# Four heads to a key transpose, read out by ScalarE's scale and bias, and a gate-up product that stays in PSUM

## The chip, the core and the metric

The kernel runs on one core of a Trainium2 chip. The metric is the device time of one execution, in microseconds (us).

## What is computed

A block of 16 batches of 256 tokens of width 256, in fp32:

```
x = x + attention(layernorm(x), keys and values from fside; ctx gives 256 more keys and values)   # 16 heads of 16
x = x + sum over 8 experts e of cw[e] * (silu(h @ w_gate[e]) * (h @ w_up[e])) @ w_down[e]          # h = layernorm(x)
```

Every expert is applied to every token (hidden width 1024); cw is a product of two softmaxes over the experts, normalised. So the expert part is by far the largest: for each group of two batches (512 tokens), 8 experts times 8 blocks of 128 hidden units.

## The kernel before

**Precision.** Most matmul operands are split into a high and a low fp32r part, and a product takes three passes (high by high, high by low, low by high). The high part is a ScalarE copy, the low part a subtraction on VectorE (DVE) or GpSimd (POOL).

**Steps and turns.** The program is one unrolled list of turns of 32 steps. In turn b the engines do the attention of batch b, prepare batch b+1, close batch b-1, and, from step 19 of turn 2 on, one expert block f in each step. There are 512 such blocks. Every engine walks the same steps in order and waits on semaphores; nothing is reordered at run time.

**One step on TensorE (PE)**, in this order: gate(f+1), six matmuls into `ps_g` (L660, shown as ps_s); up(f+1), six into `ps_u` (L660, ps_t); down(f), six into `ps_o` (L694); every fourth step the attention-times-value matmuls (L735, L737); one "misc" item by the table ITEMS; the scores of item i+8 for their maximum (L753), the transposed scores (L763).

**One step on ScalarE (ACT):** tanh of the gate into the SBUF tile `hf` (L777); one or two weight halves (L789); `h_hi`, a copy of `hf` (L782); parts of the values' split; the read-out of the misc item; the exponential `Pt` (L916). **On DVE:** (tanh+1)*gate into `hf` (L937); times up, into `hf` (L944); statistics; `h_lo` = `hf` - `h_hi` (L949); the router's small operations; in even steps `Pt_lo`, the low part of the exponentials (L1077; POOL has the others, L1237); the misc item; the negated row maximum `negmax` (L1141), which frees the one score bank. **On POOL:** low weight halves (L1172), `kstack`'s low parts, the sum over experts.

**The locks that matter here.** tanh(f+1) waits for h_lo(f), which is the last reader of `hf`. up(f+1) waits for the product (L944) of f, the last reader of `ps_u`. down(f) waits for h_lo(f). All misc items share one PSUM bank, `ps_m`, so each waits until the one before has been read out.

**Keys.** The split keys lie in `kstack` as four slots of 16 columns per head: high, low, a slot that is 1.0 in three columns, high again. A misc item "kT" transposes two heads (128 columns) for each of four key tiles into `ps_m` (L597), and one ScalarE copy of 128x512 brings it to `KTs` (L888). The ones meet three rows of `QTs` that carry the query's maximum. Eight kT items per batch stand in steps 19, 20, 25, 27, 28 of the turn before and 0, 1, 4 of the batch's own. A "qq" item does the same for the queries and ends in four ScalarE copies, two of 3x256 (L899) and two of 64x256 (L904).

Of the kernel before, what the change touches and what calls it, by code (L numbers as in the profile page):

```python
# [29 lines left out]
P = 128  # L30
# [6 lines left out]
def bass_xattn_moe_ffn_kernel(nc, x, ctx1, ctx2, Wq, bq, Wk, bk, Wv, bv, Wp, bp, w_router, w_gating,  # L37
# [52 lines left out]
    with ExitStack() as ctx:  # L90
# [130 lines left out]
        qT_ps = Count("qT_ps", 8); qT_done = Count("qT_done", 16)  # L221
        kT_ps = Count("kT_ps", 8); kT_done = Count("kT_done", 8)
        v_1 = Count("v_1", 4); v_r = Count("v_r", 4); v_2 = Count("v_2", 4); v_3 = Count("v_3", 4)
# [22 lines left out]
        class Turn:  # L246


            def __init__(self, b):
                self.b = b  # L250
                self.closed = (b - CLOSED) // GB if b >= CLOSED and (b - CLOSED) % GB == 0 else None
                self.qs_at, self.ks_at, self.ms_at = (10, 8, 5) if b == -1 else (18, 12, 13)

# [21 lines left out]
        def turns(body):  # L275

            for b in range(-2, LAST + 1):
                body(Turn(b))

        ITEMS = [(0, "kT", 5, 0), (1, "kT", 6, 0), (2, "qq", 1, 0), (3, "cT", 0, 1), (4, "kT", 7, 0), (5, "aT", 0, -1),  # L280
# [4 lines left out]

        FIRST_AT = {"cT": (1,), "xT": (2,), "kv": (4, 6), "q": (9,)}

        def q_ahead(k, d):

            return (k + 2) % PAIRS, d + (k + 2) // PAIRS  # L290

        def released(b, name, k, d):

            turn = Turn(b)
            if name == "y":
# [5 lines left out]
            count, nth = {"kT": (kT_done, k + 1), "kv": (kv_done, k + 1), "xT": (xT_l, 1), "cT": (cT_l, 1), "aT": (aT_l, 1),  # L301
                          "x2T": (x2T_l, 1), "q": (q_done, 1), "o": (x1_done, 1), "lg": (ldif_done, 1),
                          "cwT": (cwT_done, 1)}[name]
            return [(count.sem, (b + d) * count.per + nth)] if turn.has(d) else []
# [119 lines left out]
        def _(eng):  # L424
# [22 lines left out]
            def body(turn):  # L447
                for step in range(STEPS):
# [20 lines left out]
                    if step == 24 and turn.has(-1):  # L469
                        turn.wait(eng, cwT_done, -1, 1)  # L470
                        eng.dma_start(d_cw[:, bass.ds((turn.b - 1) * N, N)], cwT[:]).then_inc(cw_out.sem, 16)
# [67 lines left out]
        def _(pe):  # L539
# [21 lines left out]
            def stack_block(stack, t, pair):  # L561
                return stack[:, t * H + 2 * pair:t * H + 2 * pair + 2].rearrange("p h s d -> p (h s d)")

            def do_misc(turn, name, k, d, one, freed):
                ps = bank(one)
# [23 lines left out]
                elif name == "kT":  # L589
# [9 lines left out]
                    mm.then_inc(kT_ps.sem, 1)  # L599
                elif name == "qq":  # L600
                    if turn.has(d):
# [106 lines left out]
            def body(turn):  # L708
                for step in range(STEPS):
# [36 lines left out]
                    if turn.has(d):  # L746
                        h, qt = i // QT, i % QT
                        if i % 4 == 0:
                            turn.wait(pe, kT_done, d, h // 2 + 1)
                            turn.wait(pe, qT_done, d, 2 * (h // 2) + 2)  # L750
# [20 lines left out]
        def _(act):  # L771

            def tanh_of(f):

                act.wait_ge(g_ps, f + 1)
                wait_for(act, hl_done, f)
                act.activation(hf[:], ps_g[:], ACT.Tanh, scale=0.5).then_inc(tanh_done, 1)  # L777

            def high_of(f):

                act.wait_ge(hf_done, f + 1)
                act.activation(h_hi[f % FC][:], hf[:], ACT.Copy).then_inc(hh_done, 1)  # L782

# [16 lines left out]
            def before_ffn():  # L800
# [11 lines left out]
                           ACT.Copy).then_inc(const_ready, 1)  # L812

            def split_high(n):

                hi, raw = parts[n]
                act.wait_ge(w_in[n], 32 if n == 4 else 16)
                act.activation(hi, raw, ACT.Copy).then_inc(w_high, 1)

            def body(turn):  # L820
                for step in range(STEPS):
                    f = turn.f(step)
# [17 lines left out]
                    if step == turn.ks_at and turn.has(1):  # L840
                        turn.wait(act, kv_done, 1, QT)
                        turn.wait(act, kT_ps, 0, PAIRS)
                        act.activation(slots(kstack, 0, 0, 4, 3), heads_twice(KF), ACT.Copy).then_inc(ks_h.sem, 1)
                    if step == turn.ms_at and turn.has(1):
                        turn.wait(act, c2_in, 1, 16)
                        turn.wait(act, kT_ps, 0, PAIRS)
                        act.activation(slots(kstack, QT, 0, 4, 3), heads_twice(VF[:, QT:KC, :]),
                                       ACT.Copy).then_inc(ms_h.sem, 1)

# [35 lines left out]
                    if name == "kT":  # L885
                        turn.wait(act, kT_ps, d, k + 1)
                        turn.wait(act, t_ps, d - 1, 4 * k + 4)
                        act.activation(KTs[:, k, :], ps[:], ACT.Copy).then_inc(kT_done.sem, 1)  # L888
                    if name == "qq":
# [32 lines left out]
        def _(dve):  # L922
# [103 lines left out]
            def body(turn):  # L1026
                for step in range(STEPS):
# [6 lines left out]
                    for n in LOW_AT.get((turn.b, step), ()):  # L1034
                        split_low(n)
                    if turn.b == -1 and step == 8:
                        dve.wait_ge(b_in[0], 16)
# [32 lines left out]
                    if f is not None and f % EXPERT == EXPERT - 1:  # L1070
                        weigh_output(f, 1)
                    router_weights(turn, step)
                    d, i = item_at(step, -1)
                    if turn.has(d) and by_dve(i):
                        turn.wait(dve, exp_done, d, i + 1)
                        slot = i % RING
                        dve.tensor_tensor(Pt_lo[slot][:], Pt[slot][:], Pt[slot][:].bitcast(BF16)[:, 1::2],  # L1077
                                          ALU.subtract).then_inc(lo_dve.sem, 1)
                    name, k, d, one, _ = misc(turn, step)
# [57 lines left out]
                    if turn.has(d):  # L1137
                        turn.wait(dve, s_ps, d, i + 1)
                        if i % 4 == 0:
                            turn.wait(dve, mq_l, d, i // 4 - 1)  # L1140
                        dve.tensor_reduce(negmax[:, (i // 4) % 2, i % 4:i % 4 + 1], score_bank((turn.b + d) * STEPS + i)[:], AX.X, ALU.max,  # L1141
                                          negate=True).then_inc(max_done.sem, 1)

            turns(body)


        @block.gpsimd
        def _(pool):
# [46 lines left out]
            def body(turn):  # L1195
                for step in range(STEPS):
# [55 lines left out]
                    if step == turn.ks_at and turn.has(1):  # L1252
                        turn.wait(pool, ks_h, 1, 1)
                        pool.tensor_tensor(slots(kstack, 0, 1, 2, 1)[:, :, 0, :], heads(KF),
                                           slots(kstack, 0, 0, 1, 1)[:, :, 0, :].bitcast(F32),
                                           ALU.subtract).then_inc(ks_l.sem, 1)
                    if step == turn.ms_at and turn.has(1):
                        turn.wait(pool, ms_h, 1, 1)
                        pool.tensor_tensor(slots(kstack, QT, 1, 2, 1)[:, :, 0, :], heads(VF[:, QT:KC, :]),
                                           slots(kstack, QT, 0, 1, 1)[:, :, 0, :].bitcast(F32),  # L1260
                                           ALU.subtract).then_inc(ms_l.sem, 1)
                    f = turn.f(step)
# [36 lines left out]
```

## Time and profile before

| | |
|---|---|
| median of 3 runs | 2788.32 us (2787.05 to 2789.99) |
| the profiled execution | 2787.18 us, of it the span 2785.0 us |
| PE busy | 2719.2 us, 98% of the span |
| DVE / POOL / ACT busy | 2198.7 / 1807.1 / 1695.8 us (79 / 65 / 61%) |
| chain that ended last | PE 87%, DVE 6%, issue 3%, ACT 3% |

The profile covers one execution. A matmul's end is modelled, so records of consecutive matmuls overlap (0.39 us long, 0.23 us apart); what they cost is read from start to start. Times within the trace count from the start of the span.

### The profile page before, as it was taken

How to read it: one execution, taken by the hardware profiler on the slowest of the kernel's cores; microseconds unless marked ns; L12 is line 12 of the kernel's file. 1: busy time of each engine (PE TensorE's matmuls, PEld its weight loads, DVE VectorE, ACT ScalarE, POOL GpSimd, SP SyncE). 2: the span in 40 equal slices, each digit the busy share in tenths (PEclk: the TensorE clock that was granted, in tenths of full speed). 3: DMA queues.
4: the chain of work that ended last, by engine and by line, in shares of the span. 5: the costliest groups of instructions: out<-in, count | busy, mean ns of one | idle time of the engine just before them, and what ended most of it. 6: DMA issues, size and time to landing. Idle time of an engine off the chain costs nothing.

```text
span 2785.0 us, 47540 instructions
## 1 busy us (share of the span) xinstructions
PE 2719.2 (98%) x16416; PEld 2224.1 (80%) x16416; DVE 2198.7 (79%) x3254; ACT 1695.8 (61%) x3241; POOL 1807.1 (65%) x1886
## 2 busy tenths in 40 slices
PE   7789999999999999999999999999999999999998
PEld 5578878888888888878788787887878888888887
DVE  7977788878888788787787888878888878766665
ACT  7866566665666666566666666656666666644443
POOL 6766666666666667666676666766666666654554
PEclk8999999999999999999999999999999999999999
DMA  2113233332333323333232322323323233333332
GB/s 69 39 57 99 80 92 96 91 103 79 96 92 95 99 81 91 95 95 99 79 93 88 103 89 86 99 82 109 95 73 100 76 103 92 95 106 114 106 104 82
DMA packets 251275, 252.27 MB, mean 91 GB/s; under 512 B 15904, under 2 KB 242848, under 8 KB 251040
## 3 DMA queue, kind: packets, MB, share of 16 engines
q1 hardware_dynamic: 251040, 249.25, 29.9%
q8 instruction: 134, 2.20, 0.3%
q14 instruction: 101, 0.83, 0.1%
HBM read 240.66 MB, written 8.52 MB: 89 GB/s over the span
## 4 chain that ended last, share of the span: by engine, by line
PE 87%; DVE 6%; issue 3%; ACT 3%; POOL 1%; DMA 0%; POOLq 0%; ACTq 0%; DVEq 0%
PE ps_s L660 23%; PE ps_t L660 23%; PE ps_o L694 23%; PE ps_s L753 4%; PE ps_t L763 3%; PE ps_m L549 3%; PE ps_a L735 2%; PE ps_a L737 2%; DVE negmax L1141 1%; DVE h_lo L949 1%; DVE Pt_lo L1077 1%; PE ps_m L597 1%; PE ps_m L557 1%; DVE hf L944 1%; ACT h_hi L782 1%
## 5 line engine op out<-in xcount | busy, mean ns | idle before, releaser
L949 DVE TENSOR_TENSOR h_lo<-hf,h_hi 128x512 fp32r<-128x512 f32 x512 | 514.6, 1005 | 230.8 <-ACT h_hi L782 220.5
L782 ACT ACTIVATE h_hi<-hf 128x512 fp32r<-128x512 f32 x512 | 323.9, 633 | 522.0 <-DVE hf L944 522.0
L937 DVE SCALAR_TENSOR_TENSOR hf<-hf,ps_s 128x512 f32<-128x512 f32 x512 | 349.5, 683 | 268.5 <-ACT hf L777 265.4
L777 ACT ACTIVATE hf<-ps_s 128x512 f32<-128x512 f32 x512 | 306.0, 598 | 306.2 <-PE ps_s L660 200.9
L1172 POOL TENSOR_TENSOR wg_lo<-stage_w,wg_hi 128x512 fp32r<-128x512 f32 x256 | 338.8, 1323 | 223.2 <-ACT wg_hi L789 223.0
L1237 POOL TENSOR_TENSOR Pt_lo<-Pt 128x512 f16<-128x512 f32 x256 | 312.4, 1220 | 152.8 <-ACT Pt L916 152.5
L694 PE MATMUL ps_o<-h_hi,wd_hi 128*128 128x512 f32 x1024 | 399.9, 391 | 0.9 <-DVE h_lo L949 0.9
L694 PE MATMUL ps_o<-h_lo,wd_hi 128*128 128x512 f32 x1024 | 399.9, 391 | 0.0
L694 PE MATMUL ps_o<-h_hi,wd_lo 128*128 128x512 f32 x1024 | 398.6, 389 | 0.0
L1172 POOL TENSOR_TENSOR wd_lo<-stage_w,wd_hi 128x512 fp32r<-128x512 f32 x256 | 332.3, 1298 | 82.2 <-ACT wd_hi L789 82.0
L944 DVE TENSOR_TENSOR hf<-hf,ps_t 128x512 f32<-128x512 f32 x512 | 351.8, 687 | 35.5 <-PE ps_t L660 0.8
L916 ACT ACTIVATE Pt<-ps_t 128x512 f32<-128x512 f32 x512 | 304.2, 595 | 121.2 <-PE ps_t L763 117.2
L1172 POOL TENSOR_TENSOR wu_lo<-stage_w,wu_hi 128x512 fp32r<-128x512 f32 x256 | 366.6, 1432 | 0.0
L1141 DVE TENSOR_REDUCE negmax<-ps_s 128x1 f32<-128x512 f32 x512 | 346.2, 678 | 3.6 <-PE ps_s L753 3.5
L660 PE MATMUL ps_s<-xh,wg_hi 128*128 128x512 f32 x1024 | 323.6, 397 | 3.2 <-issue 3.2
L660 PE MATMUL ps_s<-xl,wg_hi 128*128 128x512 f32 x1024 | 319.4, 393 | 0.0
L660 PE MATMUL ps_s<-xh,wg_lo 128*128 128x512 f32 x1024 | 318.3, 392 | 0.0
L660 PE MATMUL ps_t<-xh,wu_hi 128*128 128x512 f32 x1024 | 318.0, 391 | 0.0
L660 PE MATMUL ps_t<-xh,wu_lo 128*128 128x512 f32 x1024 | 316.8, 391 | 0.0
L660 PE MATMUL ps_t<-xl,wu_hi 128*128 128x512 f32 x1024 | 315.2, 389 | 0.0
L1077 DVE TENSOR_TENSOR Pt_lo<-Pt 128x512 f16<-128x512 f32 x256 | 290.1, 1133 | 5.6 <-ACT Pt L916 5.5
L753 PE MATMUL ps_s<-KTs,QTs 128*128 128x512 f32 x512 | 235.4, 460 | 28.0 <-DVE negmax L1141 25.0
(190 smaller groups left out, 5117.6 us busy)
## 6 DMA issues: line engine op xcount, KB each, us to landing
stage_w<-in_L_ffn_w_gate_dram SPq DMA_DIRECT2D x256, 256.0 KB, 2.8
stage_w<-in_L_ffn_w_up_dram SPq DMA_DIRECT2D x256, 256.0 KB, 3.0
stage_w<-in_L_ffn_w_down_dram SPq DMA_DIRECT2D x256, 256.0 KB, 2.7
cwb<-d_cw SPq DMA_DIRECT2D x64, 256.0 KB, 3.8
X<-in_x_dram SPq DMA_DIRECT2D x32, 256.0 KB, 3.6
C<-in_fside_BxSxS_dram SPq DMA_DIRECT2D x16, 256.0 KB, 3.0
KVM<-in_ctx_dram SPq DMA_DIRECT2D x16, 256.0 KB, 2.7
d_x<-X SPq DMA_DIRECT2D x16, 256.0 KB, 2.4
```

The lines of the kernel that those rows point to most:

```text
L660: mm = pe.matmul(ps[:], wt[:, c, q * P:(q + 1) * P], tok[:, c].rearrange("p k n -> p (k n)"), start=(n == 0), stop=(n == 3 * DC - 1))
L694: mm = pe.matmul(ps_o[:, c, :], wt[:, q, c * P:(c + 1) * P], hid[:], start=(at == 0 and n == 0), stop=(at == EXPERT - 1 and n == 2))
L753: pe.matmul(score_bank(j)[:], QTs[:, h // 2 % QRING, h % 2, qt * P:(qt + 1) * P], KTs[:, h // 2, :], start=True, stop=True).then_inc(s_ps. ...
L777: act.activation(hf[:], ps_g[:], ACT.Tanh, scale=0.5).then_inc(tanh_done, 1)
L782: act.activation(h_hi[f % FC][:], hf[:], ACT.Copy).then_inc(hh_done, 1)
L937: dve.scalar_tensor_tensor(out=hf[:], in0=hf[:], scalar=1.0, in1=ps_g[:], op0=ALU.add, op1=ALU.mult).then_inc(gate_done, 1)
L944: dve.tensor_tensor(hf[:], hf[:], ps_u[:], ALU.mult).then_inc(hf_done, 1)
L949: dve.tensor_tensor(h_lo[f % FC][:], hf[:], h_hi[f % FC][:].bitcast(F32), ALU.subtract).then_inc(hl_done, 1)
L1077: dve.tensor_tensor(Pt_lo[slot][:], Pt[slot][:], Pt[slot][:].bitcast(BF16)[:, 1::2], ALU.subtract).then_inc(lo_dve.sem, 1)
L1141: dve.tensor_reduce(negmax[:, (i // 4) % 2, i % 4:i % 4 + 1], score_bank((turn.b + d) * STEPS + i)[:], AX.X, ALU.max, negate=True).then_in ...
L1172: pool.tensor_tensor(lo[:], raw_weights(n), hi[:].bitcast(F32), ALU.subtract).then_inc(wl_done, 1)
L1237: pool.tensor_tensor(Pt_lo[slot][:], Pt[slot][:], Pt[slot][:].bitcast(BF16)[:, 1::2], ALU.subtract).then_inc(lo_pool.sem, 1)
```

## The change

1. **A key transpose of four heads ("kQ"), for batches 3 to 15.** `kstack` holds only high and low (32 columns per head, the view `qkeys`), so 128 columns are four heads. The item fills `ps_m` with four heads; the slots doubled and the ones set are made while reading out. `keys_out` writes one pair of heads with four ScalarE instructions of 32x512: for each head a Copy of its 32 rows, and an Identity of the same 32 rows with `scale=high_rows` and `bias=max_rows` (one value for each partition, from SBUF), which gives ones and high. A second call in the next step (`keys_next`) writes the other pair. kQ stands in steps 12, 19, 27 of the turn before and 0 of its own. Batches 0 to 2 keep kT.
2. **The copies into the stack:** one half instead of two (L843, L847), in steps 10 and 11 instead of 12 and 13. Items o, kv, kv, xT move to steps 7, 8, 9, 11; y's second and cwT trade places (23, 24); the store of cwT moves to step 25.
3. **The product stays in PSUM:** L944 writes `ps_u` in place; h_hi and h_lo read it there. tanh(f+1) waits only for the product of f; up(f+1) waits for h_lo(f).
4. **DVE's order:** the router's operations and `Pt_lo` come last in the step, after `negmax`.

```diff
-        ITEMS = [... (8, "o", 0, -1), (9, "kv", 0, 1), (10, "qq", 3, 0), (11, "kv", 1, 1), (13, "xT", 0, 1),
+        ITEMS = [... (7, "o", 0, -1), (8, "kv", 0, 1), (9, "kv", 1, 1), (10, "qq", 3, 0), (11, "xT", 0, 1),
...
+                 (0, "kQ", 3, 0), (12, "kQ", 0, 1), (19, "kQ", 1, 1), (27, "kQ", 2, 1)]
...
+                elif name == "kQ":
+                    for t in range(KC):
+                        mm = pe.transpose(ps[:, t * P:(t + 1) * P].bitcast(F32R), quad_block(t, k), ident_r[:])
+                    mm.then_inc(kT_ps.sem, 2)
...
             def up(f):
-                wait_for(pe, hf_done, f)
+                wait_for(pe, hl_done, f)
...
             def tanh_of(f):
-                wait_for(act, hl_done, f)
+                wait_for(act, hf_done, f)
...
             def high_of(f):
-                act.activation(h_hi[f % FC][:], hf[:], ACT.Copy).then_inc(hh_done, 1)
+                wait_for(act, d_ps, DC * (f - 1))
+                act.activation(h_hi[f % FC][:], ps_u[:], ACT.Copy).then_inc(hh_done, 1)
...
+            def keys_out(turn, ps, pair, d):
+                turn.wait(act, t_ps, d - 1, 4 * pair + 4)
+                act.wait_ge(rows_ready, 2)
+                for h in range(2):
+                    src, dst = 2 * HD * (pair % 2 * 2 + h), HS * h
+                    act.activation(KTs[dst:dst + 2 * HD, pair, :], ps[src:src + 2 * HD, :], ACT.Copy).then_inc(kT_done, 1)
+                    dst = dst + 2 * HD
+                    act.activation(KTs[dst:dst + 2 * HD, pair, :], ps[src:src + 2 * HD, :], ACT.Identity,
+                                   bias=max_rows[src:src + 2 * HD, :], scale=high_rows[src:src + 2 * HD, :]).then_inc(kT_done, 1)
...
             def hidden_of(f):
-                dve.tensor_tensor(hf[:], hf[:], ps_u[:], ALU.mult).then_inc(hf_done, 1)
+                dve.tensor_tensor(ps_u[:], hf[:], ps_u[:], ALU.mult).then_inc(hf_done, 1)
...
             def low_of(f):
-                dve.tensor_tensor(h_lo[f % FC][:], hf[:], h_hi[f % FC][:].bitcast(F32), ALU.subtract).then_inc(hl_done, 1)
+                dve.tensor_tensor(h_lo[f % FC][:], ps_u[:], h_hi[f % FC][:].bitcast(F32), ALU.subtract).then_inc(hl_done, 1)
```

## Rows read from the trace of the kernel before

**Rows 1.** The page's first part: busy us (share) x instructions, by engine.
```profile
PE 2719.2 (98%) x16416; PEld 2224.1 (80%) x16416; DVE 2198.7 (79%) x3254; ACT 1695.8 (61%) x3241; POOL 1807.1 (65%) x1886
```
**Rows 2.** The waits of PE, 350 to 2350 us: us in total, times, longest.
```profile
PE ps_s L753 <- DVE negmax L1141: 16.3, 12, 1.6
```
**Rows 3.** The chain in time, steps 27 to 30 of turn 8: start, us, what.
```profile
1236.38 0.30 PE ps_m L597 x4
...
1237.20 1.40 PE ps_s L660 x6
...
1242.16 1.40 PE ps_s L660 x6
...
1246.76 1.40 PE ps_s L660 x6
...
1252.51 0.23 PE ps_s L660
```
**Rows 4.** ScalarE's timeline, turn 8, steps 19, 26 to 29: start, us, instruction.
```profile
1192.16 0.59 ACT L777 ACTIVATE hf<-ps_s 128x512 f32<-128x512 f32 x1
...
1231.75 0.78 ACT L899 ACTIVATE QTs<-ps_m 3x256 fp32r<-3x256 f32 x2 [0.68 <-PE ps_m L612]
1232.55 0.78 ACT L904 ACTIVATE QTs<-ps_m 64x256 fp32r<-64x256 f32 x2
1233.36 0.60 ACT L916 ACTIVATE Pt<-ps_t 128x512 f32<-128x512 f32 x1
1233.85 0.59 ACT L777 ACTIVATE hf<-ps_s 128x512 f32<-128x512 f32 x1
...
1235.92 0.63 ACT L782 ACTIVATE h_hi<-hf 128x512 fp32r<-128x512 f32 x1 [0.96 <-DVE hf L944]
1236.71 0.60 ACT L888 ACTIVATE KTs<-ps_m 128x512 fp32r<-128x512 f32 x1 [0.16 <-PE ps_m L597]
...
1238.64 0.60 ACT L777 ACTIVATE hf<-ps_s 128x512 f32<-128x512 f32 x1 [0.80 <-PE ps_s L660]
...
1243.60 0.60 ACT L777 ACTIVATE hf<-ps_s 128x512 f32<-128x512 f32 x1 [0.80 <-PE ps_s L660]
```
**Rows 5.** PE's timeline, turn 8: starts of gate in steps 19, 29, of up in 30.
```profile
1189.04 0.63 PE L660 MATMUL ps_s<-xh,wg_hi 128*128 128x512 f32 x2
...
1242.00 0.63 PE L660 MATMUL ps_s<-xh,wg_hi 128*128 128x512 f32 x2
...
1247.99 0.62 PE L660 MATMUL ps_t<-xh,wu_hi 128*128 128x512 f32 x2
```
**Rows 6.** DVE's timeline, step 29 of turn 8: h_lo.
```profile
1246.43 0.69 DVE L949 TENSOR_TENSOR h_lo<-hf,h_hi 128x512 fp32r<-128x512 f32 x1 [0.70 <-ACT h_hi L782]
```
**Rows 7.** DVE and PE in step 21 of turn 8, around the wait of Rows 2.
```profile
1202.83 1.53 DVE L1077 TENSOR_TENSOR Pt_lo<-Pt 128x512 f16<-128x512 f32 x1
1204.28 0.68 DVE L1141 TENSOR_REDUCE negmax<-ps_s 128x1 f32<-128x512 f32 x1
...
1205.01 0.50 PE L753 MATMUL ps_s<-KTs,QTs 128*128 128x512 f32 x1 [1.14 <-DVE negmax L1141]
```
**Rows 8.** Groups by line, whole span: busy us, mean ns of one | idle before.
```profile
L949 DVE TENSOR_TENSOR h_lo<-hf,h_hi 128x512 fp32r<-128x512 f32 x512 | 514.6, 1005 | 230.8 <-ACT h_hi L782 220.5
...
L866 ACT ACTIVATE lexp<-ldif 128x16 f32<-128x16 f32 x32 | 4.8, 198 | 0.0
```
**Rows 9.** DVE and PE near the end, steps without attention: h_lo, next up.
```profile
2704.61 1.47 DVE L949 TENSOR_TENSOR h_lo<-hf,h_hi 128x512 fp32r<-128x512 f32 x1 [0.70 <-ACT h_hi L782]
...
2705.67 0.62 PE L660 MATMUL ps_t<-xh,wu_hi 128*128 128x512 f32 x2
```
**Rows 10.** POOL's timeline, step 10 of turn 7: the sum over experts.
```profile
1145.06 3.45 POOL L1191 TENSOR_TENSOR acc<-acc,wout 128x512 f32<-128x512 f32 x2
```
**Rows 11.** SP's queue in turn 8, steps 24 and 25: the store of cwT, the first load back.
```profile
1217.02 0.30 SPq L471 DMA_DIRECT2D d_cw<-cwT  x1
...
1222.82 0.41 SPq L520 DMA_DIRECT2D cwb<-d_cw  x1
```

More of the change, by code:

```diff
@@ L57, in bass_xattn_moe_ffn_kernel @@
     DVE_LOW = (1, 3, 5, 7)
+    QUADS = PAIRS // 2
+    FIRST_QUAD = 3
     SCALE = float(HD) ** -0.5
@@ L290, in q_ahead, with by_quad, keys_done @@
             return (k + 2) % PAIRS, d + (k + 2) // PAIRS
+        def by_quad(b):
+            return b >= FIRST_QUAD
+        def keys_done(b, pairs):
+            late = max(b - FIRST_QUAD, 0)
+            return (b - late) * PAIRS + late * 2 * QT * PAIRS + pairs * (2 * QT if by_quad(b) else 1)
         def released(b, name, k, d):
             turn = Turn(b)
+            if name in ("kT", "kQ"):
+                if not turn.has(d) or by_quad(b + d) != (name == "kQ"):
+                    return []
+                return [(kT_done, keys_done(b + d, 2 * k + 2 if name == "kQ" else k + 1))]
             if name == "y":
@@ L468, in body @@
                         eng.dma_start(x1_v[:, bass.ds((turn.b - 1) * QT, QT), :], X1[:]).then_inc(x1_out.sem, 16)
-                    if step == 24 and turn.has(-1):
+                    if step == 25 and turn.has(-1):
                         turn.wait(eng, cwT_done, -1, 1)
@@ L842, in body @@
                         turn.wait(act, kT_ps, 0, PAIRS)
-                        act.activation(slots(kstack, 0, 0, 4, 3), heads_twice(KF), ACT.Copy).then_inc(ks_h.sem, 1)
+                        if by_quad(turn.b + 1):
+                            act.activation(qkeys[:, 0:QT * H, 1, :], heads(KF), ACT.Copy).then_inc(ks_h.sem, 1)
+                        else:
+                            act.activation(slots(kstack, 0, 0, 4, 3), heads_twice(KF), ACT.Copy).then_inc(ks_h.sem, 1)
                     if step == turn.ms_at and turn.has(1):
@@ L846, in body @@
                         turn.wait(act, kT_ps, 0, PAIRS)
-                        act.activation(slots(kstack, QT, 0, 4, 3), heads_twice(VF[:, QT:KC, :]),
-                                       ACT.Copy).then_inc(ms_h.sem, 1)
+                        if by_quad(turn.b + 1):
+                            act.activation(qkeys[:, QT * H:KC * H, 1, :], heads(VF[:, QT:KC, :]),
+                                           ACT.Copy).then_inc(ms_h.sem, 1)
+                        else:
+                            act.activation(slots(kstack, QT, 0, 4, 3), heads_twice(VF[:, QT:KC, :]),
+                                           ACT.Copy).then_inc(ms_h.sem, 1)
                     for o, at, d in v_at(turn):
@@ L887, in body @@
                         turn.wait(act, t_ps, d - 1, 4 * k + 4)
-                        act.activation(KTs[:, k, :], ps[:], ACT.Copy).then_inc(kT_done.sem, 1)
+                        act.activation(KTs[:, k, :], ps[:], ACT.Copy).then_inc(kT_done, 1)
+                    if name == "kQ":
+                        turn.wait(act, kT_ps, d, 2 * k + 2)
+                        keys_out(turn, ps, 2 * k, d)
+                    if keys_next:
+                        keys_out(turn, bank(keys_next[3]), 2 * keys_next[1] + 1, keys_next[2])
+                    keys_next = items[turn.b, step] if name == "kQ" else None
                     if name == "qq":
@@ L1035, in body @@
                         split_low(n)
+                    if turn.b == 0 and step == 0:
+                        in_head = ident[:].rearrange("p (a r) -> p a r", r=2 * HD)
+                        dve.tensor_reduce(high_rows[:], in_head[:, :, HD:2 * HD], AX.XY, ALU.add).then_inc(rows_ready, 1)
+                        dve.tensor_reduce(max_rows[:], in_head[:, :, 0:3], AX.XY, ALU.add).then_inc(rows_ready, 1)
                     if turn.b == -1 and step == 8:
@@ L1071, in body @@
                         weigh_output(f, 1)
[L1072 to L1078, printed above, removed]
                     name, k, d, one, _ = misc(turn, step)
@@ L1142, in body @@
                                           negate=True).then_inc(max_done.sem, 1)
+                    router_weights(turn, step)
+                    d, i = item_at(step, -1)
+                    if turn.has(d) and by_dve(i):
+                        turn.wait(dve, exp_done, d, i + 1)
+                        slot = i % RING
+                        dve.tensor_tensor(Pt_lo[slot][:], Pt[slot][:], Pt[slot][:].bitcast(BF16)[:, 1::2],
+                                          ALU.subtract).then_inc(lo_dve.sem, 1)
             turns(body)
```

30 lines of the change are left out of this document (20 added, 10 removed), and 6 rows, old and new, of the table ITEMS.

## The prediction

> **What bounds the kernel now.** First the page's busy times: PE is busy for 98% of the span, no other engine for more than 79% [rows 1]. Then PE's waits between 350 and 2350 us: there is one kind, the score matmul waiting for `negmax`, twelve times, once per turn in step 21 [rows 2]. So in steady state PE runs back to back but for one hole per turn, and the time is the sum of what PE streams. The chain gives that from start to start: a step without a misc item lasts 4.60 us (1242.16 to 1246.76), one with a kT item 4.96 (1237.20 to 1242.16), one with a qq item and the value matmuls 5.75 (1246.76 to 1252.51) [rows 3]. Last, ScalarE's and DVE's timelines, for the loop that feeds PE: gate, tanh, two DVE products, h_hi, h_lo. A faster step is worth something only while this loop keeps up.
>
> **What it saves.** (a) A kT item costs 4.96 - 4.60 = 0.36 us of PE's time: 0.30 of it are the four transposes, the rest the exposed load behind them [rows 3]. Thirteen batches have four items fewer each: 52 x 0.36 = 18.7 us, all of it on the path. (b) The hole in step 21: DVE spends 1.53 us on Pt_lo, then 0.68 on negmax, and PE starts 0.05 us after that [rows 7]. With Pt_lo and the router's work behind negmax the score bank is free earlier by more than the hole. The records give 16.3 us for the twelve [rows 2]; a matmul's record runs some 0.2 us past the point where the next could start, so I take 16.3 + 12 x 0.2 = 18.7. (c) h_lo takes 1.005 us on average with two SBUF inputs, 0.69 where it is undisturbed [rows 8, 6]. Reading `ps_u`, I take 0.69 throughout: 512 x 0.315 = 161 us off DVE. None of it is on the path, and it pays only by keeping the loop short. Together 37.4 us.
>
> **What it adds: the new lock.** up(f+1) now waits for h_lo(f), which down(f) used to wait for one product later. In a step of 4.60 us h_lo ends at 1246.43 + 0.69 = 1247.12 and the next up starts at 1247.99: a slack of 0.87 us [rows 6, 5]. From tanh (1243.60) to that end are 3.52 us [rows 4]. Near the end, where steps are 4.1 us, h_lo would end at 2704.61 + 0.69 = 2705.30 against 2705.67: 0.37 left [rows 9]. So by itself the lock costs nothing; its cover is this slack. When tanh is late, the product no longer waits for up, tanh to h_hi takes 2.07 instead of some 2.16 (1233.85 to 1235.92) [rows 4], and the slack is 0.96. No row has DVE writing PSUM. I take it as a write to SBUF. The bounds are a gain of 0.03 us in h_hi and a loss of 0.2 in the product; more would already show in the 0.37 of the last steps.
>
> **What it adds: the read-out.** One copy of 128x512 (0.60 us long, the exponential follows 0.53 after its start) [rows 4] becomes four instructions per pair of heads. Their time depends on columns, not rows, so 32x512 is as long as 128x512. And there is a second cost. Copies that change their partitions do not overlap: two of 3x256 take 0.78 us and the next starts 0.80 after the first, so 0.40 each, a full duration of 0.38 plus 0.02; full-height instructions follow each other by 0.49 at a duration of 0.60 (1233.36, 1233.85) [rows 4]. `keys_out` moves to other partitions every time, so a Copy costs 0.62. Identity with a scale and a bias from SBUF has no row. It isn't below a Copy, 0.60; above, two operands can't cost more than a whole small activation of 0.198 us [rows 8], so 0.80. I take 0.75, near the top, since both must be in before the first element. K, one `keys_out`, is 2 x 0.62 + 2 x 0.77 = 2.78 us, between 2.48 and 2.88.
>
> The Trainium skill ("ScalarE: Activation LUTs", What ACT_TABLE_LOAD costs) gives about 93 ns for each per-partition pointer operand. By it Identity would be 0.79 and K 2.86, and the sum below some 8 us higher; no row here can show it.
>
> **How late ScalarE gets.** `keys_out` stands between h_hi and the exponential, and queued behind it are the exponential and the next tanh; DVE and then PE wait for that tanh.
> First step: the read-out starts at 1236.71 and the next tanh at 1238.64, 1.93 later [rows 4]. Now it can't come before K + 0.49 (the exponential) = 3.27. Late by 1.34.
> Second step: it has no item, so PE needs 4.60. ScalarE needs 2.07 (tanh to h_hi) + 0.63 + 2.78 + 0.49 = 5.97. Late by 1.34 + 1.37 = 2.71.
> PE's stall up to the up after that is 2.71 - 0.96 = 1.75, less what that step is longer than 4.60.
> - Steps 27, 28, then 29 without item: 1.75.
> - Steps 0, 1 and 12, 13, then 2 and 14 with qq (5.75): 1.75 - 1.15 = 0.60 each.
> - Steps 19, 20, then 21: tanh already starts 1192.16 - 1189.04 = 3.12 after its gate, against 1243.60 - 1242.00 = 1.60 [rows 4, 5], so 1.52 late from the start. First step: 1.52 + (2.07 + 0.54 + 2.78 + 0.49) - 4.96 = 2.44; second: 3.81; stall 3.81 - 0.96 = 2.85, less 0.44 in every other turn, where y lengthens step 21: 2.6.
>
> Per turn 5.55 us. With 13 episodes of the first kind, 13 and 12 of the second (batch 3's lies before the expert blocks), 12.5 of the third: 22.8 + 7.8 + 7.2 + 32.5 = 70 us. With K = 2.48 the second lateness falls by 0.6 (two `keys_out`): 15 + 1 + 1 + 25 = 42. With 2.88 it rises by 0.2: 78.
>
> **What else moves.** The stack copies halve, off the path. Their low parts stand behind POOL's sum over experts, which takes 3.45 us in step 10 [rows 10], and PE needs them in step 12 instead of 19. They should come within a few tenths of PE; bound 0 to 0.5 us x 12, I add 2. Items in steps 7 to 12 now follow each other without a gap in the one bank; each is read in its own step, so nothing. SP's store of cwT goes one step later. Before, the first load of it went out 1222.82 - 1217.02 = 5.8 us after the store [rows 11]; up to 2 us of lateness in every other turn falls on step 26, a long one. Nothing. Two small reductions for the row constants run once. The start-up before the expert blocks has DVE's new order too; which way it shifts no row says, and I leave it to the range.
>
> **The sum**, against the profiled execution's 2787.2: - 37.4 + 70 + 2 = +34.6, so 2822. Two terms of it are rough on the same side: every late chain gains 0.03 us from h_hi's faster source, 104 times, 3 us. That gives 2819 for that execution and, as the median lies 1.1 higher, 2820.
>
> **Rivals.**
> *ScalarE keeps up (faster).* If the partial instructions followed each other like full ones, 0.48 apart, K is 1.9, or 2.3 with Identity's operands. Lateness in steps 27 and 28 is then 0.5 and 0.9, covered by the slack; only steps 19 to 21 stall, by 0.8 (1.6 at 2.3, and 0.7 in 27 to 29). Time 2787 - 37 + 10 to 29 = 2760 to 2779, on the median's scale 2761 to 2780. Against it is the 0.40 for 0.38 of rows 4. The point from which it decides is K of about 2.4, where the stalls equal the 37 us saved. Chance 0.18.
> *Even.* K at its lower end: 2787 - 37 + 42 + 2, some 2795; with a little more slack than I read, within 0.2%. Chance 0.15, of it 0.10 within.
> The Trainium skill ("VectorE: DVE Perf Modes", Two Vector instructions with no wait between them) holds a Vector instruction back until all before have finished when its start quadrant changes. If ScalarE follows the same rule, and its 0.40 in rows 4 looks like it, the faster rival falls.
> *The product in PSUM slows every chain.* Each 0.1 us there lengthens the lateness of all 52 episodes by 0.3: +16 us, to 2836; from 0.4 us on it stalls every one of the last hundred steps too, past 2840. DVE's reads of PSUM being as short as its SBUF work speaks against it. Chance 0.07.
> *The change doesn't remove the hole*, because in step 21 PE waits anyway, now at up: that is in the forecast, as the third kind of episode.
> *Forecast*: 2803 to 2836, chance 0.60.
>
> **Numbers.** 2820. For 8 in 10, the range leaves out most of the faster rival and half of the PSUM one: 2770 to 2838. 0.2% (5.6 us) is about what a measurement of this kernel tells from no change. Faster 0.19; within 0.11; slower 0.70.
>
> **What would show it.** PE: L597 in 208 fewer matmuls; the wait for negmax in step 21 gone; in its place waits of ps_t's first matmul (up) for h_lo, in steps 20 to 22, 29 and 30, and small ones in 2, 3, 14 and 15, some 65 to 75 us. ScalarE: keys_out rows of 0.60 and 0.75 to 0.80, each starting as the last ends; busy up by some 190 us. h_lo at 0.69. The prediction is wrong if the four start 0.5 us apart, if steps of 4.60 us stall with no keys_out near, or if the low parts of the stack come late in step 12.

## The result

The changed kernel takes 2860.12 us (median of 5 runs, 2858.87 to 2861.7) against 2788.32: slower, ratio 1.0258 [1.0244, 1.0272], +72 us. The forecast was +32 (2820), its range ended at 2838. The direction was right, and so was the cause of the largest term, a late ScalarE. Two terms that had been put at nothing were not nothing, and the stalls were a little larger than forecast.

The page of the changed kernel, parts 1 and 4, answers to [rows 1]:

```profile
PE 2739.9 (96%) x16208; PEld 2201.3 (77%) x16208; DVE 1989.4 (70%) x3256; ACT 1901.9 (67%) x3553; POOL 1713.1 (60%) x1886
...
PE 71%; ACT 11%; DVE 9%; issue 8%; POOL 1%; ACTq 0%; DMA 0%; POOLq 0%; DVEq 0%
```

PE has 208 matmuls fewer, DVE 209 us less to do, ACT 206 more. The share of PE in the chain fell from 87% to 71%: work of ACT and DVE that used to be hidden now sets the end. The waits of PE between 350 and 2350 us show where, and answer to [rows 2]:

```profile
PE ps_t L688 <- DVE h_lo L1005: 40.2, 93, 0.7
PE ps_s L688 <- DVE hf L993: 11.4, 30, 0.5
```

The wait for `negmax` is gone. In its place up waits for the low part (93 times) and gate for DVE's gate product. The span grew by 72.7 us (2785.0 to 2857.7), in two places. A steady turn (turns 4 to 14, gate start to gate start) went from 169.8 to 173.9. And the first stretch, up to the first gate of the expert blocks, went from 168.6 to 186.2. By windows, the kernel before, then the changed one (columns: busy us of PE, PEld, DVE, ACT and POOL with instructions, granted clock, DMA share, GB/s):

```profile
0.00:168.60 168.60, 126.90 (x1189) 94.71 (x1189) 139.87 (x264) 128.23 (x268) 119.50 (x195) 0.92 0.19 51
```

```profile
0.00:186.20 186.20, 133.46 (x1192) 99.42 (x1193) 136.70 (x266) 133.03 (x276) 117.05 (x195) 0.88 0.15 46
```

PE's work is the same there (1189 and 1192 instructions), spread over 17.6 us more. With the longer waits the mean granted clock fell from 0.92 to 0.88, a mean over time at 2.4 GHz and at 1.2 GHz, and PE's busy time rose by 6.6 us: part of the 17.6 are matmuls that themselves ran longer. The read-outs on ScalarE's timeline, steps 27 and 28 of turn 8, answer to [rows 4]:

```profile
1286.93 0.60 ACT L811 ACTIVATE h_hi<-ps_t 128x512 fp32r<-128x512 f32 x1 [0.31 <-DVE ps_t L1000]
1287.56 0.59 ACT L849 ACTIVATE KTs<-ps_m 32x512 fp32r<-32x512 f32 x1
1288.18 0.77 ACT L851 ACTIVATE KTs<-ps_m,max_rows,high_rows 32x512 fp32r<-32x512 f32 x1
1288.97 0.59 ACT L849 ACTIVATE KTs<-ps_m 32x512 fp32r<-32x512 f32 x1
1289.59 0.77 ACT L851 ACTIVATE KTs<-ps_m,max_rows,high_rows 32x512 fp32r<-32x512 f32 x1
1290.38 0.60 ACT L972 ACTIVATE Pt<-ps_t 128x512 f32<-128x512 f32 x1
1290.88 0.59 ACT L805 ACTIVATE hf<-ps_s 128x512 f32<-128x512 f32 x1
```

From 1287.56 to 1290.38 are 2.82 us for one `keys_out`, forecast at 2.78. Each of its instructions starts 0.62 or 0.79 to 0.80 after the one ahead of it, at durations of 0.59 and 0.77: none overlaps with the next. What follows on DVE and PE:

```profile
1293.59 0.69 DVE L1005 TENSOR_TENSOR h_lo<-ps_t,h_hi 128x512 fp32r<-128x512 f32 x1 [0.67 <-ACT h_hi L811]
```

```profile
1281.88 0.63 PE L688 MATMUL ps_s<-xh,wg_hi 128*128 128x512 f32 x2
...
1286.46 0.63 PE L688 MATMUL ps_s<-xh,wg_hi 128*128 128x512 f32 x2
...
1292.34 0.70 PE L688 MATMUL ps_s<-xh,wg_hi 128*128 128x512 f32 x2 [0.50 <-DVE hf L993]
...
1294.42 0.70 PE L688 MATMUL ps_t<-xh,wu_hi 128*128 128x512 f32 x2 [0.46 <-DVE h_lo L1005]
```

A step that was 4.60 long [rows 3] is 5.88 (1286.46 to 1292.34), because up before it waited too, and the next one is 6.54 in place of 5.75.

### The profile page after: what moved, and what is told of

It reads as the page before. It is cut to its first block, busy times and chain, and to the rows that moved or that the text cites. A ratio compares the mean times of both kernels' runs of the same rounds, so it can differ in the third digit from the quotient of the medians.

```text
span 2857.7 us, 47936 instructions
## 1 busy us (share of the span) xinstructions
PE 2739.9 (96%) x16208; PEld 2201.3 (77%) x16208; DVE 1989.4 (70%) x3256; ACT 1901.9 (67%) x3553; POOL 1713.1 (60%) x1886
## 4 chain that ended last, share of the span: by engine, by line
PE 71%; ACT 11%; DVE 9%; issue 8%; POOL 1%; ACTq 0%; DMA 0%; POOLq 0%; DVEq 0%
PE ps_t L688 20%; PE ps_o L722 19%; PE ps_s L688 17%; ACT KTs L851 3%; PE ps_m L567 3%; PE ps_s L781 3%; DVE hf L993 3%; PE ps_t L791 2%; DVE ps_t L1000 2%; ACT Pt L972 2%; ACT hf L805 2%; PE ps_a L763 2%; PE ps_a L765 2%; DVE h_lo L1005 2%; ACT h_hi L811 1%
## 5 line engine op out<-in xcount | busy, mean ns | idle before, releaser
L811 ACT ACTIVATE h_hi<-ps_t 128x512 fp32r<-128x512 f32 x512 | 306.2, 598 | 430.4 <-DVE ps_t L1000 430.4
L1233 POOL TENSOR_TENSOR wg_lo<-stage_w,wg_hi 128x512 fp32r<-128x512 f32 x256 | 332.5, 1299 | 302.8 <-ACT wg_hi L818 302.2
L1005 DVE TENSOR_TENSOR h_lo<-ps_t,h_hi 128x512 fp32r<-128x512 f32 x512 | 352.8, 689 | 206.7 <-ACT h_hi L811 198.6
L1298 POOL TENSOR_TENSOR Pt_lo<-Pt 128x512 f16<-128x512 f32 x256 | 274.7, 1073 | 270.0 <-ACT Pt L972 268.6
L1000 DVE TENSOR_TENSOR ps_t<-hf,ps_t 128x512 f32<-128x512 f32 x512 | 356.3, 696 | 42.0 <-PE ps_t L688 5.1
L688 PE MATMUL ps_t<-xh,wu_hi 128*128 128x512 f32 x1024 | 329.7, 403 | 44.8 <-DVE h_lo L1005 44.6
L1233 POOL TENSOR_TENSOR wu_lo<-stage_w,wu_hi 128x512 fp32r<-128x512 f32 x256 | 350.6, 1370 | 0.0
L688 PEld LDWEIGHTS ps_t<-xh,wu_hi 128*128 128x128 f32 x1024 | 181.7, 188 | 129.9 <-issue 64.6
L688 PEld LDWEIGHTS ps_s<-xh,wg_hi 128*128 128x128 f32 x1024 | 188.5, 188 | 69.6 <-issue 22.9
```

Source lines behind the costliest of these rows:

```text
L688: mm = pe.matmul(ps[:], wt[:, c, q * P:(q + 1) * P], tok[:, c].rearrange("p k n -> p (k n)"), start=(n == 0), stop=(n == 3 * DC - 1))
L811: act.activation(h_hi[f % FC][:], ps_u[:], ACT.Copy).then_inc(hh_done, 1)
L1000: dve.tensor_tensor(ps_u[:], hf[:], ps_u[:], ALU.mult).then_inc(hf_done, 1)
L1005: dve.tensor_tensor(h_lo[f % FC][:], ps_u[:], h_hi[f % FC][:].bitcast(F32), ALU.subtract).then_inc(hl_done, 1)
L1233: pool.tensor_tensor(lo[:], raw_weights(n), hi[:].bitcast(F32), ALU.subtract).then_inc(wl_done, 1)
L1298: pool.tensor_tensor(Pt_lo[slot][:], Pt[slot][:], Pt[slot][:].bitcast(BF16)[:, 1::2], ALU.subtract).then_inc(lo_pool.sem, 1)
```

## The experiments

Each ratio is taken against the kernel before, run beside that kernel on the same chip; its median was 2787.1 to 2788.7 us in these series, so differences of about 1 us between rows say nothing. "First gate" is the start of the first gate matmul, "turn" the mean of turns 4 to 14, both in the one profiled execution. The turns repeat well. The first gates do so less: before, e1 and e9 run the same instructions ahead of it and reach it at 167.3 to 169.9, and e2 and e8, which also run the same ones as each other, at 172.3 and 174.9. A first gate is known to some 1 to 3 us.

| kernel | median us | ratio to before | span | first gate | turn |
|---|---|---|---|---|---|
| before | 2788.3 | 1 | 2785.0 | 168.6 | 169.8 |
| changed | 2860.1 | 1.0258 [1.0244, 1.0272] | 2857.7 | 186.2 | 173.9 |
| e1 PSUM product alone | 2775.8 | 0.9951 [0.9936, 0.9966] | 2773.8 | 169.9 | 168.6 |
| e2 DVE order alone | 2773.8 | 0.9943 [0.9928, 0.9958] | 2771.6 | 172.3 | 168.4 |
| e8 both of these | 2777.3 | 0.9964 [0.9954, 0.9975] | 2775.6 | 174.9 | 168.4 |
| e3 changed, no four-head keys | 2787.3 | 0.9994 [0.9985, 1.0004] | 2785.2 | 183.5 | 168.4 |
| e4 changed, one plain read-out | 2779.6 | 0.9968 [0.9956, 0.9981] | 2777.1 | 182.2 | 168.1 |
| e5 changed, Identity as Copy | 2825.2 | 1.0136 [1.0121, 1.0151] | 2822.4 | 185.8 | 171.3 |
| e6 changed, statistics earlier | 2851.0 | 1.0229 [1.0214, 1.0245] | 2848.9 | 187.6 | 173.0 |
| e7 changed, old items to turn 1 | 2853.3 | 1.0238 [1.0222, 1.0253] | 2853.0 | 181.5 | 173.9 |
| e9 before, order from chain on | 2768.9 | 0.9927 [0.9915, 0.994] | 2766.6 | 167.3 | 168.4 |
| e10 changed, e6 and e7 | 2843.8 | 1.0195 [1.0181, 1.0209] | 2842.4 | 180.6 | 173.0 |
| e11 changed, half to DVE | 2827.0 | 1.0136 [1.012, 1.0151] | 2823.7 | 182.4 | 171.6 |
| e12 e11 with e6 and e7 | 2824.2 | 1.0125 [1.0111, 1.0139] | 2821.7 | 179.7 | 171.6 |
| e13 changed, old until the chains | 2841.0 | 1.019 [1.0173, 1.0207] | 2838.2 | 169.0 | 174.0 |

**e1: the product in PSUM alone.** On the kernel before:

```diff
-                wait_for(pe, hf_done, f)
+                wait_for(pe, hl_done, f)
...
-                dve.tensor_tensor(hf[:], hf[:], ps_u[:], ALU.mult).then_inc(hf_done, 1)
+                dve.tensor_tensor(ps_u[:], hf[:], ps_u[:], ALU.mult).then_inc(hf_done, 1)
```

(with `high_of`, `low_of` and tanh's wait as in the change.)

> The kernel before with one part of the change: the gate-up product is written back into the gate's PSUM tile, and the locks that go with it; old order of VectorE's router work, old item lists, keys transposed two heads at a time. Theory (the slack that a step has falls to 0.87 us but nothing in the old steps eats it): 2780 to 2792 us, within 0.3% of before, with the low part's subtraction at 0.69 us instead of 1.005. Rival (a product in PSUM makes each gate-up chain longer, or the lock holds TensorE): over 2800 us.

12.4 us faster, more than the theory had. The 0.31 us off each low part were not worthless: DVE's timeline in steps 20 and 21 of turn 8, to be laid beside [rows 7], has

```profile
1195.21 0.69 DVE L950 TENSOR_TENSOR h_lo<-ps_t,h_hi 128x512 fp32r<-128x512 f32 x1 [0.23 <-ACT h_hi L783]
...
1197.05 1.77 DVE L1078 TENSOR_TENSOR Pt_lo<-Pt 128x512 f16<-128x512 f32 x1
1198.74 0.68 DVE L1142 TENSOR_REDUCE negmax<-ps_s 128x1 f32<-128x512 f32 x1
```

where the kernel before had, ahead of the same `Pt_lo`,

```profile
1200.29 1.36 DVE L949 TENSOR_TENSOR h_lo<-hf,h_hi 128x512 fp32r<-128x512 f32 x1 [0.50 <-ACT h_hi L782]
```

That is 0.67 less, and in step 20 the low part took 1.86 before and 0.69 now. `negmax` comes in time and step 21 falls from 6.56 to 4.84 while 20 and 22 grow by 0.2 and 0.3. So the hole of step 21 was the end of a DVE backlog, and a shorter low part drains it as well as another order does.

**e2: DVE's order alone**, the block of `router_weights` and `Pt_lo` moved behind `negmax`, as in the change.

> The kernel before with only VectorE's order changed: the router's work and the low part of the probabilities come after the negated maximum in the steps where they stood ahead of it. Theory (the hole of step 21 closes, nothing takes its place): 18.7 us less, 2768 to 2774 us. Rival (another wait stands right behind the hole, such as the up product's for the low part of the step before): 2782 to 2790 us.

14.4 us less: inside the range that the theory gave, but short of its 18.7. The turn lost 1.43 us; the first gate came 3.7 us later, which the expectation had not.

**e8: e1 and e2 together.**

> The kernel before with the product in PSUM and VectorE's new order, no item moved and keys two heads at a time. Theory (the hole's 18.7 us go and the shorter low part adds nothing on the path): 2763 to 2774 us, the same as with the order alone within 0.2%. Rival (the smaller slack with the router's work now behind the maximum makes the up product wait in step 22): 2780 us or more.

Neither: the expected 2763 to 2774 was missed from above. The turn is that of the order alone (168.4): the two edits remove one wait between them. Against e2 it is 3.5 us slower, 0.13%, and the two intervals overlap. 2.6 us of this lie ahead of the first gate, where both run the same instructions; e8's execution had a granted clock of 0.91 there against 0.93, and PE was busy for 129.26 us against 126.02. So this is no evidence of a cost of the product in PSUM.

**e3: the changed kernel without four-head keys.**

```diff
-    FIRST_QUAD = 3
+    FIRST_QUAD = 16
```

> The changed kernel with every batch's keys still transposed two heads at a time (the four-head transposes never start); item moves, order and product in PSUM are kept. Theory A (the read-outs of the four-head transposes cost some 7 us of stall in each turn from batch 3 on, and the items moved cost a start-up of 17 us and a stall of 0.9 us in step 12 of each turn, which stay): 52 transposes come back (+18.7), some 80 us of stall at the read-outs go: 2790 to 2805 us. Rival B (the loss is the PSUM lock or the moved items, not the read-outs): 2850 us or more.

2787.3, a little below theory A's range and far from B. The whole loss sits in the four-head keys or in what they meet; what is left of the change comes out even, its gain in the turns eaten by a first gate at 183.5. Step 12 had a stall of only 0.2 here, not 0.9.

**e4: the read-out as one plain copy.** It leaves out the doubled rows and the ones.

```diff
-                for h in range(2):
-                    ...
+                act.activation(KTs[:, pair, :], ps[:], ACT.Copy).then_inc(kT_done, 4)
```

> The changed kernel with the read-out of a four-head transpose made by one plain copy of the whole tile in place of four narrow instructions; it leaves out the doubling of the rows and the ones, so the scores are not the reference's. Theory (ScalarE's 2.8 us of read-out before the next exponentials is what makes the stalls): the 32-row instructions fall to one of 0.6 us each, stalls of 70 to 85 us go, the start-up stays: 2775 to 2790 us. Rival (the four-head form costs by its place and its PSUM tile, not by ScalarE's time): over 2830 us.

80.5 us less than the changed kernel, inside the range. Read against it, in means of turns 4 to 14, the read-outs cost 1.28 + 0.79 us in steps 29 and 30, 0.86 in 2 and 3, 0.86 in 14 and 15, and 2.06 in 20 to 22: 5.85 of the 5.87 by which the two turns differ. Steps 1, 4, 25 and 28 keep the 0.36 to 0.40 that a transpose item cost.

**e5: Identity made Copy.** It leaves out the scale and the bias.

> The changed kernel with the two scale-and-bias read-outs of each four-head transpose made plain copies (it leaves out the scale and the bias, so rows that should hold ones do not). Theory (each of the two costs 0.18 us more than a copy for its two per-partition operands, and both stand ahead of the exponentials that the next two steps need): the read-outs fall from 2.82 to about 2.45 us, the lateness of both steps of each place falls by about 0.37, and about 25 to 30 us go: 2828 to 2838 us. Rival (the stall does not follow ScalarE's time one for one): over 2850 us.

34.9 us less, more than expected. ScalarE's groups by line and form, of the changed kernel and of this one:

```profile
L851 ACT ACTIVATE KTs<-ps_m,max_rows,high_rows 32x512 fp32r<-32x512 f32 x208 | 160.3, 771 | 5.4
L849 ACT ACTIVATE KTs<-ps_m 32x512 fp32r<-32x512 f32 x208 | 122.3, 588 | 14.5 <-PE ps_m L626 10.7
```

```profile
L851 ACT ACTIVATE KTs<-ps_m 32x512 fp32r<-32x512 f32 x208 | 122.6, 589 | 5.1
```

0.18 us a piece, 37.7 us of ScalarE's time, and 35 us of the kernel's: nearly one for one. Steps 29 and 30 fell by 0.74 together, and 20 to 22 by 0.74, which is 2 x 2 x 0.18 and a little; 2 and 3, and 14 and 15, had 0.86 to lose and fell by 0.6 each. So a place pays for ScalarE's lateness as a whole. A single step need not: step 30 kept its 6.53, for which see e11. The Trainium skill ("ScalarE: Activation LUTs", What ACT_TABLE_LOAD costs) gives about 93 ns for each pointer operand; 771 - 589 = 182 ns for two agrees.

**e6: the layernorm statistics one step earlier.**

```diff
-                        norm_stats(turn, -1, 9, step, X1, ...
+                        norm_stats(turn, -1, 8, step, X1, ...
```

> The changed kernel with VectorE's layernorm statistics one step earlier in each turn, so that they no longer stand between the gate-up product and its low part in step 11. Theory (the low part of step 11 is 0.9 us late because of them, and TensorE's up product of step 12 waits for it): about 10 us less, 2847 to 2853 us, step 12 back at 5.0 us. Rival (step 12 waits for GpSimd's low part of the stacked keys): unchanged, 2857 us or more.

9.1 us less; step 12 went from 5.93 to 4.97. DVE's timeline of the changed kernel, step 11 of turn 8 (its gate starts at 1189.54), then POOL's, then PE's:

```profile
1192.66 0.70 DVE L1000 TENSOR_TENSOR ps_t<-hf,ps_t 128x512 f32<-128x512 f32 x1
1193.26 1.03 DVE L1042 TENSOR_SCALAR mv<-mv 128x2 f32<-128x2 f32 x1
1194.21 0.15 DVE L1043 TENSOR_SCALAR mv<-mv 128x2 f32<-128x2 f32 x1
1194.28 1.26 DVE L1044 SCALAR_TENSOR_TENSOR mv<-mv 128x2 f32<-128x2 f32 x1
1195.46 0.54 DVE L1110 TENSOR_REDUCE avs<-ps_a 128x128 f32<-128x384 f32 x1
1195.92 0.19 DVE L1112 RECIPROCAL rsum<-ps_a 128x8 f32<-128x8 f32 x1
1196.04 0.63 DVE L1005 TENSOR_TENSOR h_lo<-ps_t,h_hi 128x512 fp32r<-128x512 f32 x1
```

```profile
1192.98 2.53 POOL L1252 TENSOR_TENSOR acc<-acc,wout 128x512 f32<-128x512 f32 x2
```

```profile
1196.82 0.70 PE L688 MATMUL ps_t<-xh,wu_hi 128*128 128x512 f32 x2 [0.72 <-DVE h_lo L1005]
```

Two instructions on 128x2 elements take 1.03 and 1.26 us. The first ends at 1194.29, where the first of POOL's two additions ends (1192.98 + 1.27 = 1194.25); the other ends with the second (1195.51). In e3 POOL came to these additions 0.4 us later in the step, and the first small one waited only for the end of the instruction ahead of them (1159.62):

```profile
1159.45 0.21 DVE L1042 TENSOR_SCALAR mv<-mv 128x2 f32<-128x2 f32 x1
1159.57 0.15 DVE L1043 TENSOR_SCALAR mv<-mv 128x2 f32<-128x2 f32 x1
1159.64 1.26 DVE L1044 SCALAR_TENSOR_TENSOR mv<-mv 128x2 f32<-128x2 f32 x1
```

That is the 0.8 us between e3's stall in step 12 and the changed kernel's. The change had made step 11 a full 1 us shorter (5.98 to 5.00, its kv item gone), so what DVE does between product and low part was no longer covered. The Trainium skill ("SBUF — State Buffer", SBUF: two separate sides) has VectorE and GpSimd take a shared pair of SBUF ports by turns, each for a whole instruction; the rows agree.

**e7: the old items in the first turns.** `ITEMS`, `ks_at`, `ms_at` and the store as before the change in turns up to 1.

> The changed kernel with the old placing of the items, of the stacked keys' copy and of the store of the weights' copy in the first two turns only. Theory (the start-up's 17.6 us come from the items packed into short steps, 4.2 in turn 0, 4.5 in turn 1, 9 in turn 2): 7 to 12 us less, 2848 to 2853 us, with the first gate product 9 us earlier. Rival (the start-up is bound by transfers that the PSUM and queue changes delay): first gate product unmoved, 2858 us or more.

6.8 us less and the first gate 4.7 us earlier: just short of the 7 to 12 that were expected, half of the 9 at the first gate, and not half of the 17.6. The effect of turn 2 stays.

**e9: DVE's new order only where a chain runs.**

```diff
+                    if f is None:
+                        router_weights(turn, step)
+                        ...
...
+                    if f is not None:
+                        router_weights(turn, step)
+                        ...
```

(the first at the old place, the second behind `negmax`.)

> The kernel before with VectorE's new order only in the steps that run an expert chain, and the old order in the steps ahead of them. Theory (of the order's effect, 18.1 us are gained in the steady turns and 3.7 lost in the short steps of the start-up, where the low part of the probabilities behind the maximum reaches TensorE late): first gate product back at 168.6 us after the start, 2769 to 2771 us. Rival (the 3.7 us are something else, such as the router's work): 2772 us or more.

2768.9, 0.9927 [0.9915, 0.994] of before: the fastest kernel of the study, by a part of the change alone. The first gate is at 167.3; the kernel before, with the same instructions up to there, had 168.6.

**e10: e6 and e7 together.**

> The changed kernel with both repairs: the layernorm statistics one step earlier from turn 2 on, and the old placing of the items in turns up to 1. Theory (the two losses are apart, 9.1 and 6.8 us when mended alone): they add up, 2842 to 2846 us. Rival (one hides the other): 2850 us or more.

16.3 us less than the changed kernel, against 9.1 + 6.8. They add.

**e11: the scale-and-bias half on VectorE.**

```diff
+                    dve.tensor_scalar(KTs[dst:dst + 2 * HD, pair, :], ps[src:src + 2 * HD, :], high_rows[src:src + 2 * HD, :],
+                                      max_rows[src:src + 2 * HD, :], ALU.mult, ALU.add).then_inc(kT_dve, 1)
```

behind `negmax`, each after ScalarE's copy of the same head.

> The changed kernel with the scale-and-bias half of each read-out given to VectorE, at the end of its step, and only the plain copies left to ScalarE. Theory (the stalls follow how late ScalarE is, and VectorE's end of the step has room): ScalarE's read-outs fall from 2.82 to some 1.2 us a step, VectorE gains 1.2 to 1.5 us in the same eight steps of a turn; 2795 to 2825 us. Rival (the low part's engine is as tight as ScalarE, so VectorE's own lateness takes the place): 2840 us or more.

33 us less, 2 us above the theory's range. DVE's group:

```profile
L1090 DVE TENSOR_SCALAR KTs<-ps_m,high_rows,max_rows 32x512 fp32r<-32x512 f32 x208 | 168.1, 808 | 7.0
```

Step 29 is cured (5.88 to 4.60), step 30 is not (6.54), nor are 20 to 22 (18.07 to 18.17). There DVE is the late one: 1.6 us of read-out stand before the next gate product, and with them `Pt_lo` or the router's work.

Step 30 lasts 6.53 to 6.54 in the changed kernel, in e5 and here, whichever engine is late. PE's starts of its gate and its up, in e5 and then in e11, beside 1292.34 and 1294.42 of the changed kernel:

```profile
1274.25 0.70 PE L688 MATMUL ps_s<-xh,wg_hi 128*128 128x512 f32 x2
...
1276.34 0.70 PE L688 MATMUL ps_t<-xh,wu_hi 128*128 128x512 f32 x2 [0.48 <-DVE h_lo L1004]
```

```profile
1272.71 0.70 PE L695 MATMUL ps_s<-xh,wg_hi 128*128 128x512 f32 x2
...
1274.79 0.70 PE L695 MATMUL ps_t<-xh,wu_hi 128*128 128x512 f32 x2 [0.46 <-DVE h_lo L1010]
```

The up follows its gate by 2.08 to 2.09 us each time, where 1.39 is the rule (1281.88 to 1283.27 in the changed kernel). Once a gate has had to wait for the gate product, the second product, `h_hi` and `h_lo` are still to come, 0.7, 0.6 and 0.7 us long, and the new lock makes the up wait for all three. With the old lock it would wait for the product alone, done at 1292.92, and could start at 1292.34 + 1.39 = 1293.73. By this estimate some 0.7 of the 0.79 us that step 30 lost belongs to the lock. No run has four-head keys with the old lock, so this is not shown.

**e12: the two repairs on top.**

> The same with the two repairs of the statistics and of the first turns as well. Theory (three independent losses): 15 to 16 us below the kernel with the halves on VectorE alone. With that kernel near 2795 this one would be at 2780 us and under the kernel before; with it at 2825, at 2810 us. Rival (the four-head form is worth having at all): under 2770 us, below the kernel before with its order alone.

Only 2.9 us of the 15 to 16 came, 2.7 of them ahead of the first gate; the turn stayed at 171.6. Step 12 did give its 0.96 back, but 13 grew by 0.47 and 14 by 0.48: the stall had let DVE catch up, and without it the halves of steps 12 and 13 make it late. Its timeline in step 13 and the PE wait behind it:

```profile
1179.78 1.64 DVE L1096 TENSOR_SCALAR KTs<-ps_m,high_rows,max_rows 32x512 fp32r<-32x512 f32 x2
1181.45 1.60 DVE L1234 TENSOR_TENSOR Pt_lo<-Pt 128x512 f16<-128x512 f32 x1
1183.08 0.69 DVE L1004 SCALAR_TENSOR_TENSOR hf<-hf,ps_s 128x512 f32<-128x512 f32 x1
```

```profile
1183.92 0.70 PE L701 MATMUL ps_s<-xh,wg_hi 128*128 128x512 f32 x2 [0.29 <-DVE hf L1004]
```

**e13: everything but the PSUM product as it was until the chains run.** e7 up to turn 2, e9's order, `FIRST_QUAD = 4`.

> The changed kernel with everything but the PSUM product as it was until the expert chains run: the old item lists, copies and store in all turns up to 2, VectorE's old order in the steps without a chain, and four-head transposes from batch 4 on in place of 3. Theory (the 17.6 us of start-up are the sum of VectorE's order, of the moved items and of the first four-head keys in short steps): first gate product at 167 to 171 us after the start in place of 186.2; one turn runs without four-head keys, which is 5.5 us less at the step lengths of the kernels with and without them (173.9 and 168.4 a turn); 2834 to 2842 us. Rival (some of the start-up's loss is the product in PSUM or lies elsewhere): first gate at 174 us or later, 2845 us or more.

The first gate is at 169.0, so the 17.6 us are accounted for as a sum (the granted clock there is 0.92 again), and the time is inside the range. How they divide between the order and the moved items is known only as well as single first gates are. The 5.5 us that the expectation allowed for a turn without four-head keys were wrong as put: only the last steps of turn 2 lost them, 3.1 us. PE's waits before the first gate, of the changed kernel and of e13:

```profile
PE ps_s L781 <- DVE negmax L1194: 7.2, 7, 2.2
PE ps_o L763 <- DVE Pt_lo L1202: 5.7, 8, 1.8
PE ps_a L763 <- DVE Pt_lo L1202: 5.3, 8, 1.2
...
PE ps_m L626 <- POOL kstack L1322: 3.9, 1, 3.9
```

```profile
PE ps_s L787 <- DVE negmax L1208: 8.5, 10, 1.5
PE ps_m L581 <- DMA C<-in_fside_BxSxS_dram: 4.3, 1, 4.3
PE ps_o L581 <- DVE X L1085: 4.1, 2, 2.2
```

The value matmuls' 11 us of waiting for `Pt_lo`, now behind `negmax`, and the 3.9 us for the stack's low part, which the first four-head item asks for in a turn of short steps, are not among e13's longest (in e13, as in the kernel before, the value matmuls' waits come to 3.3 us). These steps last 1.7 us on average, so the latency of a chain counts in them, not the sum of the work.

## Why the prediction was short

e8, e3, e4 and the changed kernel are a ladder from before, each rung adding one part. In spans (us), with the part of it ahead of the first gate:

| rung | forecast | measured | of it ahead of the first gate |
|---|---|---|---|
| order and PSUM product (before to e8) | -18.7 | -9.4 | +6.3 |
| items, copies and store moved (to e3) | +2 | +9.6 | +8.7 |
| four heads a transpose, read out plainly (to e4) | -18.7 | -8.1 | -1.3 |
| the real read-out (to changed) | +67 | +80.6 | +4.0 |
| sum | +32 | +72.7 | +17.6 |

The rungs' own gaps add up to the 41 us that were missing. The start-up shares of the first two rungs rest on e8's 174.9; by e2's 172.3, for the same instructions, they would be 3.7 and 11.2.

- **The step that failed most** is "which way it shifts no row says, and I leave it to the range". It was put at nothing, and the start-up costs 17.6 us (e13: 0.4 left when all is put back). The trace of before could have said more: from 28.5 to 168.6 us it runs turns 0 and 1 and 19 steps of turn 2, 83 steps of 1.7 us, and an item list read only against steps of 4.6 to 6 us was changed in them. The order's share is 3.7 to 6.3 us (e2 at 172.3 and e8 at 174.9, against 168.6), and e9, with the old order there, has none of it; the moved items have most of the rest.
- **"Items in steps 7 to 12 now follow each other ... so nothing"** failed too. The bank was indeed free; but emptying step 11 took the cover from DVE's statistics. This is the third rung's missing 10 us: the transposes did save 0.36 to 0.40 each, and e6 returns 9.1. The 2 us for the stack's low part were the wrong suspect: between 350 and 2350 us PE never waits for `kstack`.
- **"None of it is on the path"**, said of the shorter low part, was wrong (e1: -12.4). It didn't hurt the sum, since the same hole had been credited to the order already. The hole itself was taken right: e2's turn is 1.43 shorter, against 18.7/12 = 1.56.
- **K and the lateness** were right: 2.82 against 2.78. Copy came at 0.62 from start to start, as taken, and Identity at 0.79 to 0.80 where 0.77 was taken. tanh came 1290.88 - 1286.46 = 4.42 after its gate against 1.60 before [rows 4, 5]: late by 2.82, forecast 2.71.
- **The stalls**, counted from steps without any wait, were some 0.3 us short each: 2.07 measured where 1.75 stood, 0.86 where 0.60 stood twice, and 2.97 where 2.6 stood (20 to 22 at 18.07 against 4.59 + 4.80 + 5.71 = 15.10 without a wait). In steps 27 to 30, 0.11 is the lateness, 0.14 is PE's restart (h_lo ends at 1294.28, up starts at 1294.42), which the slack read from running rows left out; 0.07 has no cause that I can show. Of the 2.97, 0.91 stand in e4 too, with the plain read-out (16.01): against e4 the read-outs cost 2.06 there, less than the 2.6 forecast, and 5.85 in the turn against 5.55. Behind the first gate that is 76.6 for the last rung, against 67. The upper bound in the prediction was added up slightly low: with 0.2 more on each of the 50.5 episodes it is 80, not 78.
- **The rivals.** ScalarE does not keep up (0.62 and 0.79 between starts). The product in PSUM slows no chain: DVE's product takes 0.696 us into PSUM against 0.687 into SBUF, and the last steps are still 4.1 us long. The wait at step 21 did turn into up's wait. A rival that the prediction did not have is the lock making late read-outs dearer, as step 30 suggests (e11); e1 shows only that the lock costs nothing where nothing is late, and its share in the 80.6 us stays open.

## What to carry to other kernels

An edit that saves PE 0.36 us, and in return puts two read-outs of 2.8 us on a helper engine in place of two copies of 0.6, is decided by where the helper stands in the loop: add up, step by step, what lies between the chain's links on every engine, and compare with the step's length after the edit. When an item leaves a step, look at what that step was covering. And when a schedule serves both a long steady phase and a start-up with steps of a third of the length, change it in the phase that was measured; of this change, the reordering alone, kept to the steps with a chain (e9), gives 20 us.

Two edits that each remove the same wait do not add (e1, e2, e8); and removing a stall can only move it where an engine was using it to catch up (e12).

## What the hardware showed

- 32-row activations into other partitions cost as much as full-height ones and do not overlap: 0.59 long and 0.62 apart, where full-height ones follow each other by 0.49 to 0.50. VectorE's scale and add on the same 32x512 took 0.808, more than ScalarE's 0.771.
- The same subtraction on VectorE took 0.689 on average with one input in PSUM (512 of them, none over 0.696), and 1.005 with both in SBUF [rows 8], where single ones took up to 1.87.
- VectorE's instructions on 128x2 elements took 1.03 and 1.26 us where they ended when a POOL instruction ended, and 0.15 to 0.21 where none held them (e6).
